# A 3x3 and a 5x5 preactivation block on one core: mid moved between SBUF layouts, statistics from the bands, a rewritten lead, normalization on ScalarE

## The reference

```
def _gn(v, G=16, eps=1e-05):
    g = v.reshape(B_, G, C_ // G, H_, W_)
    m = jnp.mean(g, axis=(2, 3, 4), keepdims=True)
    s = jnp.var(g, axis=(2, 3, 4), keepdims=True)
    return ((g - m) / jnp.sqrt(s + eps)).reshape(v.shape)

x = x + _L0_conv_ref(_gn(x), L0_conv_weight, L0_conv_threshold)   # 3x3, padding 1
x = x + _L1_conv_ref(_gn(x), L1_conv_kernel, L1_conv_bias)        # 5x5, padding 2, plus bias
```

## Time and profile before

| | us |
|---|---|
| median of 3 runs (913.11 to 914.11) | 913.19 |
| profiled execution | 912.25 |
| its span, first to last instruction | 910.5 |
| PE busy | 788.7 |
| DVE busy | 685.2 |
| ACT busy | 324.1 |
| POOL busy | 320.4 |

### The profile page before, as it was taken

One profiled execution on the slowest core, in us unless ns is written; L12 is line 12 of the kernel. 1 busy time (PEld: TensorE's weight loads), 2 busy tenths in 40 slices (PEclk: granted clock), 3 DMA queues, 4 the chain that ended last, 5 costly groups with the idle time before them and its releaser, 6 DMA issues.

```text
span 910.5 us, 108496 instructions
## 1 busy us (share of the span) xinstructions
PE 788.7 (87%) x52262; PEld 697.5 (77%) x52262; DVE 685.2 (75%) x1050; ACT 324.1 (36%) x417; POOL 320.4 (35%) x146
## 2 busy tenths in 40 slices
PE   1544578999999999999999999999999999998874
PEld 1433366888888889898888888898888888987774
DVE  5784534988889897979798888979797979673410
ACT  0212023344443343444434444334344443443231
POOL 0300004443434344444444243434444444434332
PEclk9877678999999999999999999999999999999998
DMA  8948943898989999998989898989989687856423
GB/s 185 224 114 213 247 115 87 226 243 221 247 202 261 209 244 238 220 252 215 246 221 243 209 247 207 265 202 244 245 217 250 166 204 182 211 149 165 100 61 77
DMA packets 72927, 183.74 MB, mean 202 GB/s; under 512 B 13248, under 2 KB 13504, under 8 KB 64704
## 3 DMA queue, kind: packets, MB, share of 16 engines
q1 hardware_dynamic: 68576, 179.45, 80.6%
q10 hardware_dynamic: 4320, 3.96, 2.1%
HBM read 116.23 MB, written 67.14 MB: 201 GB/s over the span
## 4 chain that ended last, share of the span: by engine, by line
PE 51%; DVE 31%; issue 8%; DMA 3%; SPq 3%; DVEq 1%; ACTq 1%; ACT 1%; POOL 0%; POOLq 0%
PE psum L687 51%; DVE x L549 5%; DVE bn_out L563 4%; DVE mid L571 4%; DVE bn_in L475 4%; DVE mid_bands L534 3%; DMA x_own<-x_dram 2%; DVE gscale L526 2%; DVE x_lo L557 2%; DVE deviation L511 1%; DVEq L573 1%; DVE product L509 1%; SPq L207 1%; ACTq L374 1%; DVE product L513 1%
## 5 line engine op out<-in xcount | busy, mean ns | idle before, releaser
L300 POOL TENSOR_TENSOR mid<-mid,conv_out 128x512 f32<-128x512 f32 x128 | 310.1, 2455 | 553.3 <-ACT conv_out L333 540.1
L687 PE MATMUL psum<-x_hi,s 32*32 32x512 f16 x25600 | 377.1, 381 | 19.7 <-ACTq L374 9.5
L687 PEld LDWEIGHTS psum<-x_hi,s 32*32 32x32 f16 x25600 | 338.6, 88 | 50.6 <-issue 15.5
L687 PE MATMUL psum<-x,s 32*32 32x512 f16 x13824 | 232.1, 396 | 47.1 <-DVE x L549 15.9
L687 PEld LDWEIGHTS psum<-x,s 32*32 32x32 f16 x13824 | 177.7, 88 | 99.8 <-issue 57.4
L687 PE MATMUL psum<-x_lo,s_hi 32*32 32x512 f16 x12800 | 186.5, 380 | 7.1 <-issue 7.1
L687 PEld LDWEIGHTS psum<-x_lo,s_hi 32*32 32x32 f16 x12800 | 175.5, 88 | 12.9 <-issue 8.3
L557 DVE TENSOR_TENSOR x_lo<-mid_bands,x_hi 128x2560 f16<-128x2560 f32 x32 | 104.0, 3251 | 49.9 <-PE psum L687 44.5
L549 DVE TENSOR_TENSOR x<-x_bands,x 128x2304 f16<-128x2304 f32 x32 | 102.8, 3213 | 38.8 <-PE psum L687 38.8
L571 DVE SCALAR_TENSOR_TENSOR mid<-psum,unscale,x_own 128x512 f32<-128x512 f32 x128 | 87.0, 742 | 46.5 <-PE psum L687 46.1
L333 ACT ACTIVATE conv_out<-psum,bias,unscale 128x512 f32<-128x512 f32 x128 | 94.2, 769 | 52.9 <-PE psum L687 52.9
(11 more groups left out here) (74 smaller groups left out, 162.8 us busy)
## 6 DMA issues: line engine op xcount, KB each, us to landing
x_own<-x_dram SPq DMA_DIRECT2D x128, 256.0 KB, 6.8
out_dram<-mid SPq DMA_DIRECT2D x128, 256.0 KB, 4.1
mid_bands<-mid_scratch SPq DMA_DIRECT2D x96, 320.0 KB, 7.5
mid_scratch<-mid SPq DMA_DIRECT2D x120, 256.0 KB
x_bands<-x_dram SPq DMA_DIRECT2D x96, 288.0 KB, 5.5
mid_bands<-mid_scratch SPq DMA_DIRECT2D x32, 288.0 KB, 5.3
x_bands<-x_dram SPq DMA_DIRECT2D x32, 272.0 KB, 6.3
every_mv<-mv_scratch ACTq DMA_DIRECT2D x15, 256.0 KB
```

The costliest lines, as they stand in the source:

```text
L300: nc.gpsimd.tensor_tensor(m, m, conv_out[:, b, :], ALU.add).then_inc(out_added, 1)
L687: ins = nc.tensor.matmul(psum[quad(j), bank + i, :].rearrange("p (a w) -> p a w", a=A), w[quad(i), at, :], src[quad(i), A * j + dy:A * (j ...
```

## The change

1. **Mid goes from SBUF to SBUF.** `mid_scratch` is gone. `move_mid` copies each half with 16 DMAs (source quad j, bank i, to band quad i; 32 partitions x 2 KB), `move_edges` copies the halo rows of an image with 14 (32 partitions x 1 KB). `mid_bands` has three slots in place of two.
2. **Input statistics from the bands.** `stats_in` reads the 16 own rows of `x_bands`, which has six slots (two before); `x_own` has two slots (six before) and is needed only by `take_conv3`. Bands are loaded six halves ahead.
3. **Both normalizations on ScalarE**, in place, as Identity with a scale and a bias; DVE computes the bias `gshift` once per statistic. `clear_pad` stays on DVE.
4. **Rewritten lead.** Image 1's scale is made during half 0 and mid 0's during half 2; TensorE does these products and six products on constants (`keep_warm`) between the high and low passes. Image 2's statistics go through the exchange. `take_conv3` writes two pieces of 1024 elements in place of four of 512. The w5 bound moves behind half 0.
5. **Order in a common step.** ACT takes the root right after the 5x5's low weights. DVE does the group arithmetic and scale of mid ahead of `take_conv3`.

```diff
-X_SLOTS, MID_SLOTS = 6, 5
+X_SLOTS, MID_SLOTS = 2, 5
+XB_SLOTS, MB_SLOTS = 6, 3
+PIECES = 2
...
+            def move_mid(h):
+                sp.wait_ge(mid_made, PIECES * (h + 1))
+                for i in range(Q):
+                    for j in range(Q):
+                        move_rows(h, i, j, h, i, slice(0, A), 2 + A * j)
+
+            def move_edges(n):
+
+                for i in range(Q):
+                    move_rows(2 * n + 1, i, 0, 2 * n, i, slice(0, 2), 2 + A * Q)
+                    if i + 1 < Q:
+                        move_rows(2 * n + 1, i, Q - 1, 2 * n, i + 1, slice(A - 2, A), 0)
...
+            for s in range(LAG, STEPS + 1):
                 if has5(s - 1):
...
-                if has3(s + 2):
+                if has3(s + XB_SLOTS):
                     sp.wait_ge(norm1, s + 2)
-                    load_bands(x_bands, s + 2, x, 1, x_bands_in)
...
+                    load_bands(s + XB_SLOTS)
                 if has3(s):
...
+                    move_mid(s)
+                    if s % 2:
+                        move_edges(s // 2)
+                    if has3(s + X_SLOTS):
                         load_own(s + X_SLOTS)
...
+            def normalize(which, h):
+
...
+                act.wait_ge(landed[h % slots], 16 * each * (h // slots + 1))
+                act.wait_ge(scale_ready, ROOTS.index((("x", "mid")[which], h // 2)) + 1)
+                v, at = t[:, h % slots, :, :], slice(which, which + 1)
+                nc.scalar.activation(v, v, ACT.Identity, bias=gshift[:, at], scale=gscale[:, at]).then_inc(made, 1)
...
+                if has3(s + 1) and s not in (1, LAG):
+                    normalize(0, s + 1)
                 if has5(s):
                     if s == LAG:
                         act.wait_ge(w5_split, 3)
                     act.wait_ge(a5_inner, 2 * (s - LAG) + 1)
                     weights5(s5_lo)
...
+                if gathered:
+                    take_root(gathered[0])
...
+                if has5(s + 1):
+                    normalize(1, s + 1 - LAG)
                 if has5(s):
                     act.wait_ge(a5_whole, s - LAG + 1)
                     weights5(s5_hi)
-                if gathered:
-                    take_root(gathered[0])
...
+                if gathered and s > LAG:
+                    dve.wait_ge(mv_in, 16 * exchange_number(s - 1))
+                    group_stats(gathered[0])
+                    scale_of(gathered[0])
                 if has3(s):
                     take_conv3(s)
...
+            with nc.body("lead_low0", valid_engines=only):
+                mix_mean(("x", 1))
+                keep_warm(6)
+                pe.br("lead_inner3")
```

More of the change, by code:

```diff
@@ L174, in exchanged @@
         def exchanged(s):
+            if s == 2:
+                return [("x", 2)]
             if not (3 <= s < HALVES and s % 2):
@@ L568, in take_conv3 @@
                     dve.wait_ge(out_stored[h % MID_SLOTS], 16 * Q * (h // MID_SLOTS))
+                dve.wait_ge(x_own_in[h % X_SLOTS], 16 * Q * (h // X_SLOTS + 1))
                 dve.wait_ge(c3_whole, 2 * h + 2)
-                for b in range(BANKS):
-                    nc.vector.scalar_tensor_tensor(mid[:, h % MID_SLOTS, b, :], psum[:, X3_BANK + b, :], unscale[:, 0:1],
-                                                   x_own[:, h % X_SLOTS, b, :], ALU.mult, ALU.add).then_inc(mid_made, 1)
+                each = BANKS // PIECES
+                for p in range(PIECES):
+                    at = slice(each * p, each * (p + 1))
+                    nc.vector.scalar_tensor_tensor(mid[:, h % MID_SLOTS, at, :],
+                                                   psum[:, X3_BANK + at.start:X3_BANK + at.stop, :], unscale[:, 0:1],
+                                                   x_own[:, h % X_SLOTS, at, :], ALU.mult, ALU.add).then_inc(mid_made, 1)
                 dve.drain().then_inc(bank3_go, 1)
@@ L800, in _ @@
                 last3()
-                pe.br_lt(visit, 3, on_true="lead_inner3", on_false="lead_mix")
-            with nc.body("lead_mix", valid_engines=only):
+                pe.br_lt(visit, 3, on_true="lead_low", on_false="lead_next")
+            with nc.body("lead_low", valid_engines=only):
+                pe.br_eq(step, 0, on_true="lead_low0", on_false="lead_low12")
+            with nc.body("lead_low12", valid_engines=only):
+                pe.br_eq(step, 1, on_true="lead_low1", on_false="lead_low2")
+            with nc.body("lead_low2", valid_engines=only):
+                mix_mean(("mid", 0))
+                mix_variance(("mid", 0))
+                keep_warm(6)
+                pe.br("lead_inner3")
+            with nc.body("lead_low1", valid_engines=only):
+                pe.wait_ge(w_bound, 2)
+                over_partitions(X5_BANK + 1, bound[:, 1:2])
+                keep_warm(6)
+                pe.br("lead_inner3")
+            with nc.body("lead_low0", valid_engines=only):
+                mix_mean(("x", 1))
+                keep_warm(6)
+                pe.br("lead_inner3")
+            with nc.body("lead_next", valid_engines=only):
                 pe.nop().then_inc(bank3_go, -1)
```

304 lines of the change are left out of this document (143 added, 161 removed).

## The result

| | before | after |
|---|---|---|
| median (lowest to highest, 4 runs each) | 913.35 (913.11 to 914.11) | 883.93 (879.47 to 891.09) |
| profiled execution | 912.25 | 891.09 |
| its span | 910.5 | 889.3 |

The change makes the kernel faster: the ratio after to before is 0.968, 95% interval 0.961 to 0.976. The gain is 29.4 us, where 42 were forecast. The profiled execution of after is its slowest of four, so it overstates what is lost; a second profile of the same kernel stands under the experiments.

A forecast was written before the change was run, and what follows sets the result against it. TensorE was taken as the bound, its gaps as the gain: 910.5 - 23.0 (common stretch) - 17.4 (lead) - 1.6 (tail) = 868.5 us span, 871.2 as median. Forecast 860 to 878 (0.57), range 859 to 893.

The forecast's parts named there:

- common stretch: Main loop from half 4's start to half 32's: 28 halves, 688.3 us before; all 23.0 us of odd-half gaps would go.
- T(4): Start of half 4 on TensorE, 144.41 us before; forecast at 127.0, a gain of 17.4 (12 to 22).
- the tail: Three 5x5 halves at the end; half 33 should look like half 32, gaining 1.6 us (0.8 surely, up to 2.5).
- the two rivals: ScalarE late, each pair keeping about its old gaps: 894 us, chance 0.20; and lead not shortened: 884 us, chance 0.14.
- the gain of the lead: Time saved ahead of half 4's start, through the rewritten lead and first main pass: 17.4 us (12 to 22).
- the relief: Both normalizations leave VectorE for ScalarE: VectorE 21.1 to about 18 us a half, ScalarE 10.0 to 14.5.
- the price of an issue: Each move of mid or its edges on SyncE costs 0.43 us; 46 cost 19.8, making 39 of 47.5 us a pair.
- The rival in which SyncE is the bound: Above 0.62 us a move SyncE bounds the pair; at 0.77 each, 970 us in total; chance 0.07.
- The lead up to T(3): Halves 0 to 2, the 3x3 alone, ahead of the main loop; half 3 would start at 76.1 us against 90.26.
- Low weights of half 3: First main pass: ScalarE, waiting for the third image's statistics, copies these weights at 86.8; 5x5 starts at 90.5, before 102.88.
- the 5 us off: First main pass, first 5x5 product to half 4: code-fetch pauses shorten by 5 us (0 to 9) as queues are quieter.
- The lead not shortened: Rival: bands reach VectorE late, the third image's exchange holds ScalarE, half the lead gain or more goes; 884 us, chance 0.14.

The follow-up runs named there:

- the second profile: The changed kernel run and profiled once more with nothing edited: 883.34 us, ratio 0.966 to the kernel before.
- the kernel with split moves: The changed kernel with each of the 16 moves of mid per half issued as two of 32 KB: 1175.15 us in one run.
- the kernel with little loaded: The changed kernel with bands of halves 7 and 8 and own rows of half 4 cut to one row or tile: 877.81 us, ratio 0.961.

## Why the prediction was right or wrong

The forecast span was 868.5, the profiled one 889.3. The 20.8 us between them are 1.9 in the common stretch, 16.8 before T(4), and 2.1 in the tail. The median of 883.93 lies outside the forecast of 860 to 878, which had 0.57; it lies in the range of 859 to 893 because that was drawn wide enough to take in the two rivals. The direction and the common stretch were foreseen, the gain of the lead was not there.

**Common stretch: right in size, half right in its reason.** 21.1 us (22.2 in the second profile) for 23.0. The chain from the exchange to mid's high part came out as worked out: the normalization of mid at T+14.6 for T+15, the exchange used at T+8.6 and not T+11.2, since the exchange, 6.2 us in the earlier trace rows, took 3.7 here. The working said that the gaps go because VectorE and ScalarE have room, and priced the relief only. The runs give the weights: the order is necessary, the moves with what goes with them bring most, and the relief 5 to 9 us. What the working did not have is that VectorE waits 0.5 us for each exchange in the kernel after and 3.6 in the one with mid through DRAM and the same order; that the moves make this difference is argued. The relief was larger than the sum had it: VectorE came to 16.4 us a half, not 18, since x's normalization had taken it 2.30 us on average and not 1.5 or 1.6, the two low parts became 0.7 us shorter and the takeover 0.24. ScalarE came to 14.6, as worked out.

**The moves: the price of an issue was the step that failed.** I took 0.43 between 0.43 and 0.77; it is 0.63, for 64 KB and 32 KB alike, so "gives less to queue behind" was a wrong reason for the lower end. The pair came to 47.5 us for the 39 of the sum. The bound that I gave, 0.62 an issue, was worked out with 19.2 us for the rest, which measured 18.1: the true bound is 0.64, and the kernel stands on it. The rival in which SyncE is the bound missed by 0.01 to 0.02 us an issue, and its price was right in kind: the kernel with split moves pays it in full. The chance of 0.07 was too low for a margin that thin.
The 0.43 came from loads of 32 x 10 KB. A group of 16 moves took 10.1 us, so a move's latency is not paid in turn; what is paid in turn is 0.63 us at the issuing queue. The Trainium skill (DMA: Bandwidth & Descriptors, Rules for kernel authors) advises to coalesce, because transfers under 64 KB pay mostly overhead. The trace agrees in that 32 KB cost the queue as much as 64; but own rows of 256 KB cost the same too, so no limit at 64 KB shows here. Nor is a fixed cost paid in turn, which the working had put at 92 us a pair: the 46 moves took 29.4 us of issue.

**The lead up to T(3): right, in part by luck.** 76.31 (73.9 to 77.1 in the profiles of its variants) for 76.1. Two misses cancel: half 1 began at 47.94 for 45.1, since the mean product came only after a pause of 5.24 us marked issue, although its input had stood since 31.64; halves 1 and 2 made up for it (13.75 us for 14.7, and 14.62 for 16.3).

**Low weights of half 3: 93.0 on ScalarE for 86.8.** The step that failed is again the price of an issue: 30 moves took 20.4 us for 12.9, so mid's normalization waited 2.99 for its rows and the statistics of half 5 waited 3.35 for bands that stand behind those moves. The sum counted the work on VectorE (3 x 2.47) and no wait for data (and its terms add up to 86.6 for VectorE, not 86.2). Asking for the bands first took the second wait away; the first 5x5 product came 4.5 us earlier and the median fell by 8, the rest being shorter pauses, which vary by themselves.

**From there to T(4): most of the 5 us off did not come.** It took 46.5 us, and 39.8 in the second profile, for 36.5, where before had 41.5. The reason given (a pause is longer beside data) is made likely by the kernel with little loaded, but a pause of 4.87 us at a share of 0.43 speaks against it as the whole. The premise was wrong: that most data is asked for by 92. SyncE's queue ran late by the same 0.2 us an issue, so bands of 5 and 6, own rows of 3 and 4, the moves of half 2 and bands of 7 and 8 were issued between 82 and 106, just ahead of and under the pauses: the share was 1.02 between 105 and 113.6, like the 1.00 of the earlier trace rows.

**Tail: half right.** The wait fell to 2.93 as forecast, worth 0.8. The clock did not follow: a wait of 2.93 is enough for it to fall as well as not. The value taken, 1.6, counted on it; the tail took 78.3 us for the 76.2 of the sum.

**Rivals.** The lead not shortened, at 884 with 0.14, is the rival that came, half by its mechanism. The exchange did hold ScalarE, and bands were late; but they were late behind 30 moves on SyncE, not because six were asked for ahead of everything, and 3.3 to 10 us of the miss lie in the stretch with the pauses. That the median meets its number to the microsecond is luck: the runs spread from 879 to 891, and 4 us of the profiled miss lie outside the lead. ScalarE was not late in the common stretch: with its order changed back it is, and then the loss is 44 us and not 23, as VectorE waits in turn.

## What to carry to other kernels

A queue that issues many small DMAs is an engine with a price per instruction: count it, read the price from the same kind of transfer, and look at what stands behind the burst, not only at the transfers in it. Where an exchange of statistics comes in the middle of a loop, the place of its steps in each engine's order decides first; here the order alone brought nothing, and the relief and the moves without it made the kernel 19 us slower than before. Where the same kernel's runs spread by 12 us, profile it twice before explaining a difference in one stage.

## What the runs showed of the hardware

- An issue on SyncE of a copy from SBUF to SBUF costs 0.63 to 0.64 us in the common stretch, for 64 KB and for 32 KB alike (up to 0.70 in groups of the lead and of the kernel with split moves); own rows of 256 KB cost as much (2.54 for four), the bands between 0.48 and 0.77, the outputs 0.9.
- The granted clock fell behind some of the waits of 2.93 us in the tail and not behind others (5.75, 7.38 and 6.97 us in one run for the same 400 products; 16 of 36 such waits in 13 profiles), and behind none of three in the one profile where 2.05 us of the wait were filled.
- Small VectorE steps on 128x1 take 0.16 us. Beside GpSimd's addition those that read two tensors take 0.47 to 1.21 and those that read one still 0.14 or 0.15. Where VectorE is full at a half's turn this puts 2.7 us on the path.
- The first run through the main loop's code pauses TensorE at every 127 or 128 products, 0.2 to 7.2 us each; the first of five was missing in nine of the eleven profiles of after and its variants.
